# A wavelet attention, expert and recurrent kernel: planned gaps of TensorE filled, its order set by longest path, and the layer norms' statistics joined on VectorE

## The reference

```python
x = x + attn_a(layernorm(x))     # q, k, v, 16 heads; products q*k shifted by d*tau, d = 1..1024, tau = 0..3,
                                 # summed per head, times softmax gains, times v shifted alike; gate; out projection
x = x + ffn(layernorm(x))        # 8 experts, the best one per token: gelu(x @ W1[e] + b1[e]) @ W2[e] + b2[e]
x = x + attn_b(layernorm(x))     # h_t = tanh(h_{t-1} @ A.T + x_t @ B.T), y_t = h_t @ C.T over 512 steps, then a layer norm
x = x + ffn(layernorm(x))        # the same experts again
```

## Time and profile before

| what | us |
|---|---|
| three runs | 1426.97, 1428.18, 1420.13 |
| median | 1426.97 |
| the profiled execution: its span (the page gives no other time of its own) | 1436.4 |
| mean granted TensorE clock, share of full speed | 0.858 |
| busy: TensorE 1170.8 (82%), VectorE 796.3 (55%), GpSimd 788.6 (55%), ScalarE 651.3 (45%) | |

### The profile page before, as it was taken

How to read it: one execution, slowest core, us unless ns; L and a number is a source line. 1 busy time by engine, 2 the same in 40 slices (tenths; PEclk the granted TensorE clock), 3 DMA queues, 4 the chain that set the end, 5 groups by cost and what they waited for, 6 DMA issues and landing times. The chain is left out here.

```text
span 1436.4 us, 32831 instructions
## 1 busy us (share of the span) xinstructions
PE 1170.8 (82%) x9942; PEld 881.1 (61%) x9942; DVE 796.3 (55%) x1723; ACT 651.3 (45%) x2050; POOL 788.6 (55%) x1274
## 2 busy tenths in 40 slices
PE   3877886888888899789988899887899998995580
PEld 2644554566565666466655666676787777785570
DVE  4878788889966777576788647542122301240110
ACT  2233332465544664455554436363564344562250
POOL 2645458563776748862748844876315642324504
PEclk9989987999988998889999759788995567998895
DMA  4700001221221212111112221233332324444542
GB/s 126 213 1 0 1 1 47 61 65 58 86 66 44 64 44 70 51 51 38 44 46 86 60 63 46 77 97 105 108 104 77 98 83 123 118 132 121 146 116 60
DMA packets 117638, 107.58 MB, mean 75 GB/s; under 512 B 15540, under 2 KB 88541, under 8 KB 117469
## 3 DMA queue, kind: packets, MB, share of 16 engines
q1 hardware_dynamic: 106704, 88.01, 21.5%
q0 software_dynamic: 8192, 16.79, 3.9%
q10 hardware_dynamic: 2573, 0.69, 0.2%
HBM read 76.73 MB, written 28.70 MB: 73 GB/s over the span
## 5 line engine op out<-in xcount | busy, mean ns | idle before, releaser
L799 POOL TENSOR_TENSOR acc<-acc,term 128x512 f32<-128x512 f32 x219 | 281.5, 1286 | 71.9 <-DVE term L1341 54.8
L1160 PE MATMUL bank<-w,hT 128*128 x1088 | 217.5, 324 | 22.1 <-ACT hT L985 13.9
L1341 DVE TENSOR_TENSOR term<-bank,V 128x512 f32<-128x512 f32 x251 | 168.0, 684 | 67.2 <-PE bank L1110 44.0
L1005 ACT ACTIVATE hid<-bank 128x16 f32<-128x16 f32 x512 | 93.0, 182 | 243.6 <-PE bank L1187 203.0
L985 ACT ACTIVATE hT<-bank,b1T 128x128 f32<-128x128 f32 x544 | 165.2, 370 | 79.2 <-PE bank L1147 65.2
L839 POOL DMA_INDIRECT back<-sorted_y,slot_i x128 | 125.1, 978 | 135.8 <-DMA back<-sorted_y,slot_i 44.2
L1160 PEld LDWEIGHTS bank<-w,hT 128*128 128x128 f32 x1088 | 173.9, 221 | 41.1 <-issue 35.6
L1187 PEld LDWEIGHTS bank<-hid,abcT 128*32 128x32 f32 x4096 | 88.6, 116 | 162.2 <-ACT hid L1005 83.2
L1312 DVE SCALAR_TENSOR_TENSOR made<-bank,qkvb,K 128x512 f32<-128x512 f32 x251 | 176.2, 742 | 17.8 <-PE bank L1083 7.2
L1187 PE MATMUL bank<-hid,abcT 128*32 128x16 f32 x4096 | 138.6, 201 | 38.3 <-ACT hid L1005 37.1
L1147 PE MATMUL bank<-xTb,w1b 128*128 128x128 f32 x864 | 166.8, 321 | 3.2 <-ACT xTb L973 3.0
(11 more groups left out here) (177 smaller groups left out, 2153.4 us busy)
## 6 DMA issues: line engine op xcount, KB each, us to landing
w1b<-in_W SPq DMA_DIRECT2D x130, 256.0 KB
K<-in_W SPq DMA_DIRECT2D x54, 256.0 KB
xsb<-sorted_x SPq DMA_DIRECT2D x184, 64.0 KB
sorted_y<-ysb SPq DMA_DIRECT2D x136, 64.0 KB
X<-in_x SPq DMA_DIRECT2D x64, 64.0 KB
out_x<-X SPq DMA_DIRECT2D x64, 64.0 KB
sorted_x<-K SPq DMA_DIRECT2D x14, 256.0 KB, 3.6
sorted_y<-made SPq DMA_DIRECT2D x48, 64.0 KB
```

The source lines that it names most:

```text
L799: nc.gpsimd.tensor_tensor(acc[:], acc[:] if k > 1 else term[0][:], term[k % NTERM][:], ALU.add).then_inc(S["terms_added"], 1)
L1005: nc.scalar.activation(hid[n % 2][:, cs], bank[6 + n % 2][:, cs], ACT.Tanh).then_inc(S["h_ready"], 1)
L1160: last = nc.tensor.matmul(bank[SLOT_BANK[place(n)]][:, 0:D], tile(hT[place(n)], c), w2[:, ds(second[n] + c * D, D)], start=(c == 0), stop= ...
L1341: V_.tensor_tensor(term[k % NTERM][:], bank[2 + k % 2][:], V[:, at:at + CW], ALU.mult).then_inc(S["terms_ready"], 1)
```

## The change

The computation is the same. The change has three parts.

1. `timeline` is written anew. Every piece has two costs now, the time after which the next one on its engine may begin and the time it takes; hops between engines, the switch of ScalarE's table and the landing of DMAs have figures of their own. For each piece the longest chain of work from it to the end is summed, and of the pieces that can begin now (or within 0.15 us) the one with the longest chain is placed. The waits in the program are those of before, except that fillers wait for another reader.
2. `fillings` looks at every gap of the plan. It sums the columns that TensorE works through in a stretch before each piece, and puts fillers into the gap ahead of the piece where the sum is short of 6000, one per 0.11 us of gap at most. Bank 0 may take fillers as well. There were 486 fillers at 83 places; there are 2114 at 666 places, 439 of them directly ahead of a step of the recurrence.
3. `statistics` on VectorE goes on, after the four `bn_stats`, with four `bn_aggr` (mean and variance of 128 elements), a `tensor_scalar` that adds epsilon to the variance and one that turns the mean's sign. Before the first `bn_aggr` and before the first `tensor_scalar` it waits for its own operation. `moments` on GpSimd keeps two of its 13 operations: the power and one product.

The core of the diff (the tables of costs are cut to a line):

```diff
-PE_PACE = 0.93
-IDLE_US, FILL_US, FILL_SHARE, FREE_US = 0.5, 0.15, 0.65, 1.0
...
+PACE = dict(
+    counts=(0.45, 0.60), gatep=(0.87, 1.02), kproj=(0.87, 1.02), vproj=(0.87, 1.02), qproj=(0.87, 1.02), logit=(0.82, 0.97),
...
+def hop(todo, x, y):
+
+    e, f = todo[x].engine, todo[y].engine
+    return todo[x].took + HOP_OF.get((x[0], y[0]), HOP.get((e, f), 0.08)) + LANDS.get(x[0], 0.0)
...
+        to_go[key] = max((hop(todo, key, y) + to_go[y] for y in followers[key]), default=todo[key].took)
...
+            if r <= now + LOOK_US:
+                choice = (DAWDLE * max(0.0, r - now) - to_go[key], key)
+                if best is None or choice < best[0]:
+                    best = choice, max(r, now)
...
-        if best and end and BEGIN[key] - best[0] > IDLE_US:
-            out[key] = int((BEGIN[key] - best[0]) * FILL_SHARE / FILL_US), best[1], best[2]
...
+SPAN_US, TARGET, FILL_US, FILL_COLS, FREE_US = 3.4133, 6000, 0.11, 256, 0.3
...
+        lack = TARGET - sum(c for _, c in recent) - columns_of(*key)
+        most = int((at - since) / FILL_US)
+        if end and lack > 0 and most > 0:
+            late = sum(since + FILL_US * j > stop - SPAN_US for j in range(most))
+            times = most - late + min(late, -(-lack // FILL_COLS))
+            out[key] = times, b, x
...
-                op(total, m_even, m_odd, ALU.add)
-                op(diff, m_even, m_odd, ALU.subtract)
-                step.done(op(sq, q_even, q_odd, ALU.add))
-                step.wait()
...
-                step.done(op(rs, var, mhalf, ALU.pow))
-                step.wait()
-                return op(nm, neg, rs, ALU.mult)
+            def moments(mv, rs, nm):
+                var, neg = mv.rearrange("p (t s) -> p s t", s=2)[:, 0, :], mv.rearrange("p (t s) -> p s t", s=2)[:, 1, :]
+                step.done(nc.gpsimd.tensor_tensor(rs, var, nums[:, 0:1].broadcast_to(list(rs.shape)), ALU.pow))
                 step.wait()
+                return nc.gpsimd.tensor_tensor(nm, neg, rs, ALU.mult)
...
-            def statistics(src, raw, ready):
+            def statistics(src, mv, ready):
                 for c in range(TPC):
                     last = V_.bn_stats(raw[:, 6 * c:6 * c + 6], tile(src, c))
-                last.then_inc(ready, 1)
+                step.done(last)
+                step.wait()
+                for c in range(TPC):
+                    last = V_.bn_aggr(mean_var[:, 2 * c:2 * c + 2], raw[:, 6 * c:6 * c + 6])
+                step.done(last)
+                step.wait()
+                by_kind, to = (t.rearrange("p (t s) -> p s t", s=2) for t in (mean_var[:], mv))
+                V_.tensor_scalar(to[:, 0, :], by_kind[:, 1, :], EPS, None, op0=ALU.add)
+                V_.tensor_scalar(to[:, 1, :], by_kind[:, 0, :], -1.0, None, op0=ALU.mult).then_inc(ready, 1)
```

More of the change, by code:

```diff
@@ new lines @@
+HOP = {("ACT", "PE"): 0.13, ("ACT", "DVE"): 0.03, ("PE", "ACT"): 0.05, ("PE", "DVE"): 0.04, ("DVE", "PE"): 0.06, ("DVE", "ACT"): 0.03}
+HOP_OF = {("state", "step"): 0.05, ("step", "state"): 0.07, ("turned", "hidden"): 0.05, ("hidden", "gelu"): 0.13,
+          ("gelu", "result"): 0.13, ("result", "yadd"): 0.14, ("yadd", "turn"): 0.15, ("slots", "scatter"): 0.29}
+LANDS = {"scatter": 1.75, "gather": 1.70}
+BEGINS = {"PE": 23.5, "ACT": 23.5, "DVE": 22.5, "POOL": 12.0, "SP": 22.0}
+TABLE_US, TURN_US, LOOK_US, DAWDLE = 1.283, 0.11, 0.15, 50.0
@@ new lines, in cost @@
+def cost(what, n, k):
+    if what in ("hidden", "result"):
+        us = 0.222 * HC / parts(n)
+        return us, us + 0.17
+    if what == "gelu":
+        us = 0.25 * HC / parts(n)
+        return us, us + 0.12
+    if what == "spread" and terms(n)[k].g not in (0, 1):
+        return 0.87, 1.02
+    if what == "spread":
+        return 0.31, 0.47
+    if what == "scale" and k == 2:
+        return 0.21, 0.31
+    if what == "xmom":
+        us = 0.35 + 0.27 * TPC * (STATS_GROUP[n][1] - STATS_GROUP[n][0])
+        return us, us
+    return PACE[what]
@@ L192, in past, with pieces, piece @@
+def pieces():
+    todo = {}
+    def piece(engine, what, n, k, after, bank0=None):
+        todo[what, n, k] = Piece(engine, *cost(what, n, k), [x for x in after if x is not None], bank0)
     def past(what, n, k=0):
         return (what, n, k) if n >= 0 else None
-    URGENT, USUAL = 0.0, 1.0
     for i in range(CHUNKS):
@@ L376, in timeline @@
-    engines = ["SP", "POOL", "ACT", "PE", "DVE"]
-    left = {key: len(x[3]) for key, x in todo.items()}
+            piece("PE", "step", c, k, [("state", c, k - 1) if k else past("state", c - 1, CT - 1), ("rxb", c, 0) if k == 0 else None])
+            piece("ACT", "state", c, k, [("step", c, k), past("ry", c - 2) if k == 0 else None])
+        piece("PE", "ry", c, 0, [("state", c, CT - 1)])
+        piece("DVE", "rres", c, 0, [("ry", c, 0)])
+        piece("DVE", "rstats2", c, 0, [("rres", c, 0), past("rmom2", c - 2)])
@@ L378, in timeline @@
+def timeline():
+    todo = pieces()
     followers = {key: [] for key in todo}
     for key, x in todo.items():
-        for y in x[3]:
+        for y in x.after:
+            assert y in todo, (key, y)
             followers[y].append(key)
-    can, free = {e: {} for e in engines}, {e: 0.0 for e in engines}
+    to_go, left = {}, {key: len(x) for key, x in followers.items()}
+    ends = [key for key, m in left.items() if m == 0]
+    while ends:
+        key = ends.pop()
+        to_go[key] = max((hop(todo, key, y) + to_go[y] for y in followers[key]), default=todo[key].took)
+        for y in todo[key].after:
+            left[y] -= 1
+            if left[y] == 0:
+                ends.append(y)
+    engines = ["PE", "ACT", "DVE", "POOL", "SP"]
+    left = {key: len(x.after) for key, x in todo.items()}
+    can, free = {e: {} for e in engines}, dict(BEGINS)
@@ L422, in timeline, with columns_of @@
             seen[key[0]] = place[key] + 1
-    turn = {key: k for k, key in enumerate(key for key in order["PE"] if todo[key][5] == 1)}
+    turn = {key: k for k, key in enumerate(key for key in order["PE"] if todo[key].bank0 == 1)}
     return order, place, turn, begin, todo
 ORDER, PLACE, TURN, BEGIN, WORK = timeline()
+SPAN_US, TARGET, FILL_US, FILL_COLS, FREE_US = 3.4133, 6000, 0.11, 256, 0.3
+def columns_of(what, n, k):
+    if what in ("xT", "pT", "rT", "rows"):
+        return 960
+    if what in ("kproj", "vproj", "qproj", "gatep", "rxb", "ry"):
+        return 2048
+    if what == "spread":
+        return 512 if terms(n)[k].g in (0, 1) else 2048
+    if what in ("hidden", "result"):
+        return 512 * HC // parts(n)
+    if what == "reduce":
+        return 600 * len(batches(n)[k])
+    return dict(turn=240, logit=1760, reduce2=512, out=2560, plog=128, counts=1024, step=85)[what]
@@ new lines, in fillings @@
+        most = int((at - since) / FILL_US)
[3 more added lines that the diff above has]
+            out[key] = times, b, x
+            recent += [(since + FILL_US * j, FILL_COLS) for j in range(times) if since + FILL_US * j > stop - SPAN_US]
+        recent.append((at, columns_of(*key)))
+        if key in TURN:
+            last_of[0] = CLOSED_BY[what], n, k
+        elif what == "turn":
+            last_of.pop(SLOT_BANK[place(n)])
```

349 lines of the change are left out of this document (161 added, 188 removed).

## The result

| | before | after |
|---|---|---|
| median of the runs | 1425.4 us (1420.1 to 1428.2, 4 runs) | 1371.2 us (1370.8 to 1373.1, 4 runs) |
| ratio to before | | 0.965, 95% interval 0.959 to 0.971 |
| span of the profiled execution | 1436.4 us | 1371.0 us |
| mean granted clock of TensorE | 0.858 | 0.962 |
| TensorE, VectorE, GpSimd busy | 1170.8, 796.3, 788.6 us | 1235.4, 832.0, 676.3 us |

What follows compares the result with a forecast made beforehand. No engine was full: a three-engine chain bound the first block, TensorE at half clock the recurrence, then a fixed 174 us chain. 1436.4 - 64 - 17 - 25 - 40 + 32 + 0, less 9.4, gave 1313 us (range 1235 to 1420).

Steps and rivals of the forecast that it cites:

- the clock, late: TensorE from 800 to 1285 us: more fillers keep the clock up and win back half-clock time, -64 us (0 to -86).
- the fillers' own time: TensorE: 1628 more fillers at 0.13 us are 212 us, 15% of it taken as cost, +32 us (0 to +212).
- The estimate of 0.54 us a step: Recurrence on TensorE: step 0.18, one expert matmul 0.23 and a filler 0.13 make 0.54 us where 0.82 was.
- The order: Outside the last slots: longest chain first closes idle time in the first block and recurrence, -40 us.
- The last 23 slots: Behind the last ranking: output stores no longer stand ahead of token loads, so slots stand closer, -25 us (-10 to -33).
- The statistics: Layer norms: 129 us less of GpSimd, 60 us more of VectorE; +13 and -13 make 0 us (-20 to +40).
- The early clock: TensorE up to 800 us: a third of what the half clock costs there comes back, -17 us (0 to -52).
- The clock stays down: Slower rival: TensorE's clock doesn't rise and fillers hold up what stands behind them, 1468 us; chance 0.11.
- VectorE becomes the bound: First block: VectorE's 38 us more all show and the order closes no gap there, 1408 us (1370 to 1420); chance 0.20.
- forecast case: Whole kernel: the terms hold about as summed, 1260 to 1370 us; chance 0.50.
- The order brings more: Whole kernel: nearly all clock terms, the tail and 60 us of order, hardly a filler on the path, 1223 us; chance 0.15.
- nothing comes of it: Whole kernel: real waits differ from the plan, so gaps lie elsewhere; within 0.5% of 1427 us; chance 0.04.

Runs made afterwards that it cites:

- e5: The kernel before with the new statistics alone, in its old lists with its 486 fillers: 1400.9 us, ratio 0.987.
- e7: The changed kernel (new order and statistics) with the old rule for fillers, 770 of them, 23 ahead of steps: 1358.0 us, ratio 0.954.
- e8: The changed kernel with the old statistics, their cost told to the planner, so lists and fillers (2092) made anew: 1361.5 us, ratio 0.958.
- s1: The changed kernel again, unedited, run beside the narrow-filler kernel: 1373.1 us.
- r3: The changed kernel without the 568 fillers directly ahead of steps, run beside the change on a chip without pauses: 1338.0 us, ratio 0.942.
- e6: The kernel before with the new rule for fillers alone (1184 for 486), old order and old statistics: 1423.2 us, ratio 1.000.
- r2: The changed kernel without any of its 2114 fillers, run beside the change on a chip without pauses: 1394.7 us, ratio 0.973.
- s2: The changed kernel with the 568 fillers ahead of steps at 128 columns for 256, run beside the change: 1357.0 us.
- r4: The changed kernel with the old statistics in lists not made for them, on a chip without pauses: 1406.8 us, ratio 0.990.
- set 1: Four edits of the change or the kernel before, on the chip with pauses, beside the kernel before (1432.4 us) but not the change: 1429.5 to 1531.0 us.
- set 3: The change (1373.9 us) beside reruns without fillers, without those ahead of steps, and with old statistics, on a chip without pauses: 1394.7, 1338.0, 1406.8 us.
- e4: The kernel before's timeline and order with the new statistics and new filler rule (1184 fillers), on the chip with pauses: 1429.5 us, ratio 0.995.
- n1: The changed kernel with the 568 fillers ahead of steps at 128 columns for 256, on the chip with pauses: 1500.2 us, ratio 1.052.

## Why the prediction was right and wrong

| term | forecast | measured | by |
|---|---|---|---|
| statistics | 0 (-20 to +40) | -21 | before to e5, same chip |
| order, the last slots with it | -65 | -43 | e5 to e7, same chip; 284 fillers more and a clock of 0.906 for 0.885 are in it |
| clock and fillers together | -49 | +13 | e7 to the change |
| sum | -114 | -51 | (54 measured) |

The terms depend on the path on which the parts are added. By way of e8 (before to e8, e8 to s1) order and fillers together are -61 and the statistics +12.

**The step that failed** is the pair "the clock, late" with "the fillers' own time": -64 and -17 for the clock, +32 for the fillers. The clock itself was forecast rightly, even too low. What was wrong is to price the two apart. From e7 to the change the clock between 800 and 1285 us goes from 0.85 to 0.96, about 107 us of half clock (twice 0.11 times 485), by the forecast's own 41% worth 44 us. For it stand 603 fillers in the stretch instead of 107 (L1099 of the change, L1069 of e7):

```profile
800.00:1285.00 485.00, 162.12 (x603) 100.40 (x603) 0.96 0.34 96
```

```profile
800.00:1285.00 485.00, 15.79 (x107) 13.81 (x107) 0.85 0.35 99
```

496 more at 0.13 us each are 64 us of an engine that is busy for 93% (e7) and 96% (the change) of the stretch. If all lay on the path, 20 us more would be lost than the clock gives back; 53 of the 496 stand in the gap ahead of the last job, and the recurrence took 6.6 us more. Beside r3 the two can be weighed by what a step shows: 249 fillers at 0.11 are 27 us, and a clock of 0.97 for 0.88 in the recurrence gives 21 us back (52 us less of half clock, at 41%), so 6 us net of loss where 7.3 were measured. The forecast put 15% of the fillers' time on the path, reasoning from gaps that the plan had. Ahead of steps it is 0.11 of 0.13, about 85%, in the recurrence. The chain of the page has 165 us of fillers, 60% of 2114 times 0.13. In a stretch in which TensorE decides there are no gaps that are "really there", and 568 of the fillers stood in just that stretch or in the steps that run beside the first block. A larger share could have been read ahead: the earlier trace rows had TensorE at 94.8 of 100 us busy, though at half clock.

**The estimate of 0.54 us a step** was the second half of the same mistake. It added 0.18, 0.23 and 0.13. But the same pieces give 0.64 for the 0.82 us of the earlier trace rows, which has two matmuls: 0.18 us stood there that the sum of parts did not hold. With it 0.72 comes out, which is what the trace of the change has, and the 0.61 of r3 holds 0.20 more than its parts as well. The kernel before even had a floor above 0.54: two steps with nothing between them (TensorE) are 0.56 us apart, of which TensorE waits 0.30 for the tanh.

```profile
542.27 0.26 PE L1187 MATMUL bank<-hid,abcT 128*32 128x16 f32 x8 [0.30 <-ACT hid L1005]
542.83 0.25 PE L1187 MATMUL bank<-hid,abcT 128*32 128x16 f32 x8 [0.30 <-ACT hid L1005]
```

A sum of parts should have been held against a row that it must explain first.

**The order** brought 43 us of 65. The last 23 slots went as said: 72.4 to 45.9 us between first and last, 26 less where 25 was forecast; but 7 us more lie behind them (42.8 to 49.6, of which 5 were counted) and 4 more ahead, so the part behind the last ranking gained 16 to 18. The recurrence gained 40 (e5 to e7) where the forecast had 40 for everywhere. The first block, whose waits of 152 us were to bound that gain, lost 14 (918.7 to 932.9). GpSimd has a wait there that the kernel before hasn't, the first sum of a chunk on the chunk before's `out`, beside the one on VectorE's terms that fell from 152.3 to half:

```profile
POOL acc L855 <- PE bank L1176: 98.0, 8, 19.6
...
POOL acc L855 <- DVE term L1409: 73.1, 26, 18.5
```

Together 171 us (97.4 and 65.8 in e7), where e5 waited 173.8 us for the terms alone: the wait changed its name. Whether it costs these 14 us was not tried.

**The statistics** cost VectorE what was said: 0.67 us a block (1.46 less 0.79) where 0.75 was taken, and GpSimd lost 112 us where 129 was. That they come to nothing was wrong by 21 us in the old order. The half with "a third of VectorE's 38 us on the path" did not appear: e5 has its last residual 5.5 us ahead of e6. The half with the shorter layer norm was then too small: the recurrence goes from 353.2 (e6) or 347.0 (the profiled before) to 332.8 us. That each layer norm there hangs on GpSimd's result would explain it, but is argued and not shown, and e6 differs from e5 in its fillers too. The Trainium skill (Perfetto Trace Analysis, Optimizing Scalar/DVE Operations) has about 60 ns of overhead for an operation of VectorE on SBUF and says that the profiled latency is about twice that; six times 0.12 is 0.72, an estimate from it, and the trace agrees with 0.67. The first figure alone, as the prediction's sentence on the page used it, gave half.

**The early clock**: 0.92 to 0.99 and no gain in the first block, for the same reason. r3 keeps 0.98 there and is 18.5 us faster with fewer fillers; r2, at 0.82 with none, is 65 us slower than r3.

**The rivals.** "The clock stays down" fell: 0.96. "VectorE becomes the bound" had its sign, the last residual at 940.0 us, and the 1371 us measured lie just within its 1370 to 1420 and just outside the forecast case's 1260 to 1370. That is luck, for its mechanism is refuted by e5, r3 and s2, all with the new statistics and residuals at 919 to 923 us. The sign was badly chosen: the kernel before had 942.4 in a trace with pauses, and about 924 without them (e6). "The order brings more" fell, "nothing comes of it" too. The slower rival's point, fillers ahead of steps hold up what stands behind them, was right in kind beside a clock that rose; the two together were no rival of mine, and they are what happened.

## What to carry to other kernels

Filler matmuls pay where the tensor engine waits for something: here 1546 of them brought 42 to 57 us, all of it in the first block. Ahead of work that is ready they cost their duration, here 36 us for 568, also where they lift the clock; in a stretch in which the engine is busy anyway, price the clock's return and the fillers' time against each other before adding one, and halve the fillers first. An edit that undoes one part of a planned order measures the mismatch too (r4 against e8), so plan anew or say so. And run the very kernel that is being edited beside every set: the kernel before was beside set 1 and showed nothing, and without the change itself in set 3, set 1 would have told a false story of three large effects.

## What was not expected of the hardware

On one chip the same files take 103 to 158 us longer: no fillers 1394.7 and 1497.3, none ahead of steps 1338.0 and 1495.6, old statistics 1406.8 and 1531.0, narrow fillers 1357.0 and 1500.2. The kernel before takes 1432.4 and 1422.8 there, and 1419.2 to 1422.0 elsewhere, so it loses 10 us at most. e4, with the old order, took 1429.5 there and was run nowhere else; e5, which differs from it in fillers alone, took 1400.9 elsewhere, so e4 may well have lost some. The five largest waits of n1 that no engine or transfer of this core ends (the profile calls such a releaser remote; 31 times and 104 us in all). The trace of s2, the same kernel, has none:

```profile
ACT hid L1061 <- remote: 57.3, 19, 8.3
DVE made L1381 <- remote: 21.1, 4, 6.3
DVE ysb L1517 <- remote: 6.2, 1, 6.2
DVE X L1419 <- remote: 6.1, 1, 6.1
ACT made L1041 <- remote: 5.3, 3, 2.4
```

The first of them in time, on VectorE in the middle of products whose inputs had been there (n1), and the same place in s2 without it:

```profile
242.55 2.06 DVE L1381 SCALAR_TENSOR_TENSOR made<-bank,qkvb,K 128x512 f32<-128x512 f32 x3
248.25 2.07 DVE L1381 SCALAR_TENSOR_TENSOR made<-bank,qkvb,K 128x512 f32<-128x512 f32 x3 [3.64 <-remote]
```

```profile
242.55 4.03 DVE L1381 SCALAR_TENSOR_TENSOR made<-bank,qkvb,K 128x512 f32<-128x512 f32 x6
246.50 0.68 DVE L1415 SCALAR_TENSOR_TENSOR acc<-th,acc 128x512 f32<-128x512 f32 x1
```

The kernel before has such waits as well in its profiled execution, 28 times and 80 us in all, the two largest being

```profile
ACT hid L1005 <- remote: 27.8, 13, 5.0
DVE ysb L1448 <- remote: 16.8, 3, 6.1
```

What pauses the engines, and why kernels in the tighter order of the change lose 103 to 158 us where the looser one loses 10 at most, stays open. So does the time of the change itself on that chip, where it was not run: by its four neighbours it would be near 1500 us there, slower than the kernel before. All verdicts above on what a part is worth are from the sets without pauses and hold for those.
